# Writing the gate's x half into PSUM on ScalarE, with another order of steps and another tail

## The chip, the cores and the metric

The kernel runs on one core of a Trainium2 chip. The metric is the device time of one execution in microseconds; smaller is better. Engines are named as in the profile: PE is TensorE's matmul, PEld its weight load, DVE is VectorE, ACT is ScalarE, POOL is GpSimd, SP is SyncE, which issues all transfers here.

## What is computed

A batch of 8 sequences of 100 rows attends over 722 context rows, a gate mixes the result into x, and an RMS norm closes. All is float32.

```python
memory_proj = jnp.einsum('bme,de->bmd', memory, W_mem)                 # 8 x 722 x 1024
scores = jnp.einsum('bnd,bmd->bnm', hidden_states, memory_proj) / jnp.sqrt(jnp.float32(D))
attn = jax.nn.softmax(scores, axis=-1)
memory_context = jnp.einsum('bnm,bmd->bnd', attn, memory_proj)         # 8 x 100 x 1024
gate_input = jnp.concatenate([hidden_states, memory_context], axis=-1)
gate = jax.nn.sigmoid(jnp.einsum('bnf,df->bnd', gate_input, W_gate) + b_gate)
fused = hidden_states + gate * memory_context
return _rmsnorm(fused, norm_w)
```

## The kernel before

Features lie on partitions (8 tiles of 128), the 800 rows (8 x 100) on columns. Every float32 product is made as three matmuls of rounded operands: high by high, high by low, low by high (`three`, L287). ScalarE makes each high part, VectorE the low part.

The program has four parts. First q is made from x (L310). Then `step` (L365) runs once per batch: scores, softmax, the transposed probabilities, the context product, and between them, to fill PE's waits, the x half of the gate for feature tile b (`gate_x`, L355), which is saved to `acc[:, b, :]` (`save_gate`, L603 on ScalarE, L794 on VectorE). Then `mc_block` (L431) makes the memory context mc. Last comes the gate phase, which the change is about.

**The gate phase** goes through a written list `STEPS` (L30), (feature tile t, first column, last column): first (0, 0, 512) and (0, 512, 800), then tiles 1 to 7 of columns 0 to 512, then tiles 1 to 7 of columns 512 to 800. There are 16, numbered 0 to 15; `LAST` is 15, and `END0` is 8, the last with 512 columns. I call steps 9 to 15 the late ones. In each:

- PE (`gate_mc`, L455) makes the mc half with 24 matmuls into PSUM bank 4 or 5 in turn.
- VectorE (`gate_sum`, L866) adds the x half from `acc` and writes `gate`; ScalarE (`sigmoid`, L679) applies the sigmoid in place; VectorE multiplies by mc (`gate_times`, L872) and adds x (`fuse`, L878), which writes `acc`.
- ScalarE (`finish`, L694) squares the result and multiplies it by the norm's weight (`weigh`); VectorE (`sum_squares`, L859) adds the squares up.
- PE's step n waits for `gate_summed` of step n-2, since it uses that bank again (L460).

Step 15 is an exception. Its x half was never saved: the last batch's `gate_x` left columns 512 to 800 in PSUM bank 7 (`GLB`, `keep=True`), and PE adds to it there.

The weights of tile t+2 are split into high and low parts at step t (`SPLIT_AT`, `split_gate_w`). For the first 512 columns the norm's factor is spread over the partitions by two small PE jobs inside steps 10 and 11 (`mean_first`, `inverse`), and VectorE applies it in `output` (L890), two tiles in each of steps 11 to 14. The output of the late columns is turned on PE in three chunks of 96 rows (`turn`, L490; 8 transposes each), since they leave the chip as rows. Then follow their means (L512, L513), the root on POOL (L954), the scaling into rows on ScalarE and VectorE (L719, L938) and three transfers (L280).

Of the kernel before, what the change touches and what calls it, by code (L numbers as in the profile page):

```python
# [5 lines left out]
B, N, D = 8, 100, 1024  # L6
# [15 lines left out]


# [6 lines left out]
STEPS = [(0, 0, FIRST), (0, FIRST, R)] + [(t, 0, FIRST) for t in range(1, KD)] \  # L30
# [9 lines left out]
def build(nc, xT, ctxT, ctxN, w_mem, w_gate_x, w_mem_t, w_gate_mc, b_gate, norm_w, outT, out_rows):  # L40
# [4 lines left out]
    with top:  # L45
# [73 lines left out]
        G2B, RIB, GLB = 4, 3, 7  # L119
# [4 lines left out]
        def gate_bank(n):  # L124
            r0, r1 = STEPS[n][1:]
            return bank(G2B + n % 2, r1 - r0) if n < LAST else bank(GLB, r1 - r0, P, r0 - FIRST)
# [43 lines left out]
        gate_summed = sem("gate_summed")  # L170
# [115 lines left out]
        def _(pe):  # L286
# [68 lines left out]
            def gate_x(slot, k0, k1, keep):  # L355
                for k in range(k0, k1):
                    if keep:
                        outs = [bank(GXB, FIRST), bank(GLB, R - FIRST)]
                        stream = [(act_hi[:, k, r0:r1], act_lo[:, k, r0:r1]) for r0, r1 in ((0, FIRST), (FIRST, R))]
                    else:  # L360
                        outs, stream = [bank(GXB, H), bank(GXB + 1, H)], halves(act_hi, act_lo, k)
                    last = three(outs, w_tile(slot, k), stream, k == 0, k == KD - 1)
                return last

            def step(b, slot, cuts, keep=False):  # L365


                def fill(i):
                    if cuts[i] < cuts[i + 1]:
                        last = gate_x(slot, cuts[i], cuts[i + 1], keep)  # L370
                        if cuts[i + 1] == KD:
                            last.then_inc(w_used, 1)
# [75 lines left out]
            pe.wait_ge(gx_saved, 2 * B - 1)  # L448
# [6 lines left out]
            def gate_mc(n, after=None, work=None):  # L455

                t, r0, r1 = STEPS[n]
                pe.wait_ge(w_lo_done, J_G2 + 1 + t)
                if 2 <= n < LAST:
                    pe.wait_ge(gate_summed, n - 1)  # L460
                for k in range(KD):
                    if n == 0:
                        pe.wait_ge(mc_lo_done, k + 1)
                    done = three([gate_bank(n)], w_tile(W_HOME[t], k), [(act_hi[:, k, r0:r1], act_lo[:, k, r0:r1])],
                                 k == 0 and n < LAST, k == KD - 1, onto=n == LAST)
                    if k == after:
                        work()
                done.then_inc(gate_made, 1)
# [21 lines left out]
            def turn(i, t0, t1):  # L490

                at = FIRST + i * CHUNK
                for t in range(t0, t1):
                    done = nc.tensor.transpose(bank(2 * i + t // 4, P, CHUNK, t % 4 * P), acc[:, t, at:at + CHUNK],
                                               ident[:, :])
                return done
# [9 lines left out]
            pe.wait_ge(out_done, KD)  # L506
            turn(1, 0, KD - 1)
            turn(2, 0, KD - 1)
# [8 lines left out]
            for i in range(ROWS2):  # L517
                turn(i, KD - 1, KD).then_inc(turned, 1)
# [3 lines left out]
        def _(act):  # L522
# [84 lines left out]
            def step(b, slot, more):  # L607
# [25 lines left out]
                if not more:  # L633
                    act.wait_ge(w_used, J_GX + 1 + b)
                    nc.scalar.activation(acc[:, b, 0:FIRST], bank(GXB, FIRST), ACT.Copy).then_inc(gx_saved, 1)
# [25 lines left out]
            def split_gate_w(t):  # L661
# [4 lines left out]
                else:  # L666
                    free = (gate_made, 2)
# [11 lines left out]
            def sigmoid(n):  # L679
                t, r0, r1 = STEPS[n]  # L680
                part = gate[:, n % 2, 0:r1 - r0]
                if n < LAST:
                    act.wait_ge(gate_summed, n + 1)
                else:
                    act.wait_ge(gate_made, n + 1)
                nc.scalar.activation(part, part if n < LAST else gate_bank(n), ACT.Sigmoid,  # L686
                                     bias=bias_t[:, t:t + 1]).then_inc(gate_done, 1)

# [14 lines left out]

            for n in range(LAST + 1):
                if n in SPLIT_AT:
                    split_gate_w(SPLIT_AT[n])
                if n == END0 + 1 or n == LAST:
                    finish(n - 1)
                    sigmoid(n)
                else:  # L710
                    sigmoid(n)
                    if n > 0:
                        finish(n - 1)
            act.wait_ge(late_squared, 1)
            weigh(LAST)
            for i in range(ROWS2):
                act.wait_ge(late_rooted, 1)
                act.wait_ge(turned, i + 1)
                nc.scalar.activation(row_out[:, i * D:i * D + BANK], bank(2 * i, BANK, CHUNK), ACT.Copy,  # L719
# [4 lines left out]
        def _(dve):  # L724
# [74 lines left out]
            def step(b, slot, more):  # L799
# [18 lines left out]
                if more:  # L818
# [3 lines left out]
                      q_hi[:, :, bass.ds(b * N, N)]).then_inc(at_lo_done, 1)  # L822
                if more:
# [81 lines left out]
            gate_sum(END0 + 1)  # L905
# [5 lines left out]
            gate_sum(END0 + 2)  # L911
            sum_squares(END0 + 1)
            gate_times(END0 + 2)
            fuse(END0 + 2)
# [20 lines left out]
            for i in range(ROWS2):  # L935
                dve.wait_ge(late_rooted, 1)
                dve.wait_ge(turned, i + 1)
                nc.vector.tensor_scalar(row_out[:, i * D + BANK:(i + 1) * D], bank(2 * i + 1, BANK, CHUNK),  # L938
# [47 lines left out]
```

## Time and profile before

| | before |
|---|---|
| median of 3 runs | 306.95 us (306.56 to 307.0) |
| profiled execution | 307.06 us |
| its span | 305.3 us |
| around the span | 1.76 us |
| PE busy | 293.8 us, 96% |
| DVE busy | 171.4 us, 56% |
| ACT busy | 150.9 us, 49% |
| DMA share of the 16 engines, queue 1 | 44.1% |

The span is what the trace shows from the first to the last instruction. PE is busy from 4 us to 289 us with no gap that counts, so the remaining idle time lies at the two ends. A row of the timeline gives start, length (from first start to last end for several instructions), engine, line and operation, then in brackets how long the engine was idle before it and who ended that.

### The profile page before, as it was taken

What the parts mean: (1) busy time and instruction counts of PE and PEld (TensorE: products, weight loads), DVE (VectorE), ACT (ScalarE), POOL (GpSimd) and SP (SyncE); (2) the same over time, 40 slices, a digit from 0 to 9 for tenths busy, and PEclk for the clock granted to TensorE, in tenths of its full rate; (3) what the DMA queues carried; (4) which work ended last, traced back from release to release, by engine and by line L of the source; (5) the groups of instructions that cost most, each with busy time, mean ns of one, the idle gap of its engine ahead of it and who ended that gap; (6) DMA issues with size and microseconds to landing.
All of it is one profiled execution on the core that took longest, in us unless ns stands there. A gap on an engine that the chain in (4) does not pass through costs nothing.

```text
span 305.3 us, 4189 instructions
## 1 busy us (share of the span) xinstructions
PE 293.8 (96%) x1647; PEld 272.4 (89%) x1647; DVE 171.4 (56%) x248; ACT 150.9 (49%) x217; POOL 2.6 (1%) x8
## 2 busy tenths in 40 slices
PE   8999999999999999999999999999999999999970
PEld 7999999898989989898998889999888888899860
DVE  2758555566675656668565514433474673466752
ACT  5638337473654837365483515554554452435322
POOL 0000000000000000000000000000000000010000
PEclk9999999999999999999999999999999999999976
DMA  6996382625828295482824102292143200001325
GB/s 211 402 402 217 128 316 77 202 104 157 292 84 275 109 266 190 153 292 77 280 110 163 49 19 71 92 409 76 61 144 133 70 0 1 2 0 46 138 93 155
DMA packets 18352, 46.31 MB, mean 152 GB/s; under 512 B 1520, under 2 KB 2288, under 8 KB 18336
## 3 DMA queue, kind: packets, MB, share of 16 engines
q1 hardware_dynamic: 18336, 46.09, 44.1%
q8 instruction: 11, 0.18, 0.2%
q14 instruction: 5, 0.04, 0.0%
HBM read 42.80 MB, written 3.28 MB: 151 GB/s over the span
## 4 chain that ended last, share of the span: by engine, by line
PE 86%; issue 8%; DVE 2%; ACT 1%; DMA 1%; DVEq 0%; POOL 0%; POOLq 0%
PE ps L292 61%; PE ps L408 11%; PE ps L384 10%; PE ps L398 1%; PE ps L415 1%; DMA acc<-xT 1%; PE ps L317 0%; DVE square_sum L864 0%; ACT gate L686 0%; DVEq L45 0%; DVE gate L869 0%; DVE acc L881 0%; POOL rms L952 0%; PE ps L320 0%; POOLq L45 0%
## 5 line engine op out<-in xcount | busy, mean ns | idle before, releaser
L292 PE MATMUL ps<-act_hi,w_hi 128*128 128x400 f32 (+2 forms) x268 | 79.4, 347 | 0.0
L292 PE MATMUL ps<-act_hi,w_lo 128*128 128x400 f32 (+2 forms) x268 | 78.7, 344 | 0.0
L292 PE MATMUL ps<-act_lo,w_hi 128*128 128x400 f32 (+2 forms) x268 | 78.7, 344 | 0.0
L292 PEld LDWEIGHTS ps<-act_hi,w_hi 128*128 128x128 f32 x268 | 49.0, 188 | 3.2 <-DVE act_lo L726 0.2
L292 PEld LDWEIGHTS ps<-act_lo,w_hi 128*128 128x128 f32 x268 | 49.4, 188 | 2.2
L292 PEld LDWEIGHTS ps<-act_hi,w_lo 128*128 128x128 f32 x268 | 49.4, 188 | 2.1
L726 DVE TENSOR_TENSOR w_lo<-w_stage,w_hi 128x1024 fp32r<-128x1024 f32 (+2 forms) x23 | 26.0, 1131 | 22.8 <-ACT w_hi L530 21.5
L726 DVE TENSOR_TENSOR cn_lo<-cn_stage,cn_hi 128x1536 fp32r<-128x1536 f32 (+2 forms) x24 | 28.6, 1217 | 5.3 <-ACT cn_hi L549 5.2
L686 ACT ACTIVATE gate<-gate,bias_t 128x512 f32<-128x512 f32 (+1 forms) x15 | 9.6, 637 | 38.4 <-DVE gate L869 38.4
L726 DVE TENSOR_TENSOR ct_lo<-ct_stage,ct_hi 128x1444 fp32r<-128x1444 f32 x16 | 25.8, 1653 | 0.5 <-ACT ct_hi L541 0.5
L530 ACT ACTIVATE w_hi<-w_stage 128x1024 fp32r<-128x1024 f32 x20 | 21.0, 1054 | 8.2 <-PE ps L292 6.2
L625 ACT ACTIVATE pc<-ps,row_inv 100x512 f32<-100x512 f32 x8 | 5.5, 689 | 33.9 <-PE ps L408 33.9
L541 ACT ACTIVATE ct_hi<-ct_stage 128x1444 fp32r<-128x1444 f32 x16 | 21.7, 1408 | 0.0
L384 PE MATMUL ps<-ct_hi,qb_hi 128*100 128x362 f32 x64 | 21.4, 334 | 0.0
L384 PE MATMUL ps<-ct_lo,qb_hi 128*100 128x362 f32 x64 | 21.0, 328 | 0.0
L384 PE MATMUL ps<-ct_hi,qb_lo 128*100 128x362 f32 x64 | 21.0, 328 | 0.0
L609 ACT ACTIVATE probs<-ps,neg_top 100x722 f32<-100x722 f32 x8 | 6.9, 866 | 27.2 <-DVE neg_top L804 27.2
L726 DVE TENSOR_TENSOR act_lo<-mc,act_hi 128x800 fp32r<-128x800 f32 x8 | 8.0, 994 | 20.4 <-ACT mc L658 20.4
L408 PE MATMUL ps<-cn_hi,pt_hi 128*100 128x512 f32 (+1 forms) x48 | 18.9, 394 | 0.0
L408 PE MATMUL ps<-cn_hi,pt_lo 128*100 128x512 f32 (+1 forms) x48 | 18.9, 394 | 0.0
L408 PE MATMUL ps<-cn_lo,pt_hi 128*100 128x512 f32 (+1 forms) x48 | 18.9, 393 | 0.0
L869 DVE TENSOR_TENSOR gate<-ps,acc 128x512 f32<-128x512 f32 (+1 forms) x15 | 8.7, 580 | 17.1 <-PE ps L292 17.1
(99 smaller groups left out, 449.0 us busy)
## 6 DMA issues: line engine op xcount, KB each, us to landing
ct_stage<-ctxT SPq DMA_DIRECT2D x16, 722.0 KB, 9.4
cn_stage<-ctxN SPq DMA_DIRECT2D x8, 768.0 KB, 5.5
cn_stage<-ctxN SPq DMA_DIRECT2D x8, 512.0 KB
w_stage<-w_gate_x SPq DMA_DIRECT2D x8, 512.0 KB, 8.0
w_stage<-w_gate_mc SPq DMA_DIRECT2D x8, 512.0 KB, 3.5
x_again<-xT SPq DMA_DIRECT2D x1, 3200.0 KB, 11.7
acc<-xT SPq DMA_DIRECT2D x6, 400.0 KB, 7.1
w_stage<-w_mem_t SPq DMA_DIRECT2D x4, 512.0 KB, 5.5
```

The lines of the kernel that those rows point to most:

```text
L292: done = nc.tensor.matmul(o, wgt, stream[h][part], start=first and wgt is wh and part == 0, stop=last and wgt is wl, skip_group_check=onto)
L384: done = nc.tensor.matmul(bank(h, MH + 1, N), lhs[:, k, :], rhs[:, k, at:at + MH + 1], start=k == 0 and part == 0, stop=k == KC - 1 and pa ...
L398: done = nc.tensor.transpose(o, probs[:, t * P:t * P + rows], ident[0:N, 0:N])
L408: done = nc.tensor.matmul(bank(PCB, C, N), lhs[0:rows, t, :], rhs[0:rows, t, :], start=t == 0 and part == 0, stop=t == MT and part == 2)
L415: done = nc.tensor.transpose(bank(PTB5, N, P, c * N), pc[:, c * P:(c + 1) * P], ident[0:N, 0:N])
L530: nc.scalar.activation(w_hi[home][:, :], w_stage[:, slot, :], ACT.Copy).then_inc(w_hi_done, 1)
L541: nc.scalar.activation(ct_hi[:, 2 * s:2 * s + 2, :], ct_stage[:, 2 * s:2 * s + 2, :], ACT.Copy).then_inc(ct_hi_done, 1)
L609: nc.scalar.activation(probs[:, :].rearrange("p (h m) -> p h m", h=2), scores, ACT.Exp, bias=neg_top[:, :], scale=float(D) ** -0.5, accum_ ...
L625: nc.scalar.activation(pc[:, :], bank(PCB, C, N), ACT.Copy, scale=row_inv[:, :]).then_inc(pc_scaled, 1)
L686: nc.scalar.activation(part, part if n < LAST else gate_bank(n), ACT.Sigmoid, bias=bias_t[:, t:t + 1]).then_inc(gate_done, 1)
L726: return nc.vector.tensor_tensor(out, whole, hi.bitcast(F32), ALU.subtract)
L869: nc.vector.tensor_tensor(gate[:, n % 2, 0:r1 - r0], gate_bank(n), acc[:, t, r0:r1], ALU.add).then_inc(gate_summed, 1)
```

## The change

1. **The seed.** For steps 2 to 15, ScalarE copies the x half `acc[:, t, r0:r1]` into the PSUM bank (`seed`), and PE's 24 matmuls add to it (the first has `start=False`). VectorE's `gate_sum` stays for steps 0 and 1 only. The sigmoid of steps 2 to 15 reads PSUM and writes `gate`; it waits for `gate_made` and for `fused` of two steps before. PE's step n waits for `seeded` of its bank. `seed(n+2)` stands on ScalarE behind `sigmoid(n)`.
2. **Step order.** (1, 0, 512) comes second and (0, 512, 800) third, so both banks are written over their full 512 columns by a matmul group that starts fresh, before the first seed.
3. **The last batch.** `gate_x` is the same for all batches, bank 7 is no longer kept, tile 7 is saved by both engines, and PE's loop covers batches 2 to 7 in three turns, where it covered 2 to 5 in two, with 6 and 7 written out.
4. **VectorE's order.** `fuse(n)` comes before `sum_squares(n-1)`.
5. **The tail.** Chunk 1 is turned into banks 2 and 7 and chunk 2 into banks 4 and 3 (`TURN`). Only chunk 2 waits for `out_done`. All 8 transposes of chunk 2 stand behind the means.

```diff
-STEPS = [(0, 0, FIRST), (0, FIRST, R)] + [(t, 0, FIRST) for t in range(1, KD)] \
+STEPS = [(0, 0, FIRST), (1, 0, FIRST), (0, FIRST, R)] + [(t, 0, FIRST) for t in range(2, KD)] \
     + [(t, FIRST, R) for t in range(1, KD)]
...
+TURN = ((0, 1), (2, 7), (4, 3))
...
-            with pe.Fori(1, B // 2 - 1) as i:
+            with pe.Fori(1, B // 2) as i:
                 step(2 * i, 0, CUTS)
                 step(2 * i + 1, 1, CUTS)
-            step(B - 2, 0, CUTS)
-            step(B - 1, 1, CUTS, keep=True)
...
-            pe.wait_ge(gx_saved, 2 * B - 1)
+            pe.wait_ge(gx_saved, 2 * B)
...
-                if 2 <= n < LAST:
-                    pe.wait_ge(gate_summed, n - 1)
+                if n >= 2:
+                    pe.wait_ge(seeded, n - 1)
...
-                                 k == 0 and n < LAST, k == KD - 1, onto=n == LAST)
+                                 k == 0 and n < 2, k == KD - 1, onto=n >= 2)
...
             pe.wait_ge(weighted, LAST)
             turn(0, 0, KD - 1)
-            pe.wait_ge(out_done, KD)
             turn(1, 0, KD - 1)
-            turn(2, 0, KD - 1)
             pe.wait_ge(summed, LAST)
             pe.wait_ge(late_squared, 1)
...
             pe.wait_ge(weighted, LAST + 1)
-            for i in range(ROWS2):
-                turn(i, KD - 1, KD).then_inc(turned, 1)
+            turn(0, KD - 1, KD).then_inc(turned, 1)
+            turn(1, KD - 1, KD).then_inc(turned, 1)
+            pe.wait_ge(out_done, KD)
+            turn(2, 0, KD).then_inc(turned, 1)
...
-                if n < LAST:
+                if n < 2:
                     act.wait_ge(gate_summed, n + 1)
                 else:
+                    act.wait_ge(fused, n - 1)
                     act.wait_ge(gate_made, n + 1)
...
+            def seed(n):
+                t, r0, r1 = STEPS[n]
+                act.wait_ge(gate_done, n - 1)
+                nc.scalar.activation(gate_bank(n), acc[:, t, r0:r1], ACT.Copy).then_inc(seeded, 1)
...
             for n in range(END0 + 1):
-                gate_sum(n)
+                if n < 2:
+                    gate_sum(n)
                 if n in SPLIT_AT:
                     split_gate_w(SPLIT_AT[n])
                 gate_times(n)
+                fuse(n)
                 if n > 0:
                     sum_squares(n - 1)
-                fuse(n)
...
-            for n in range(END0 + 3, LAST):
-                gate_sum(n)
-                sum_squares(n - 1)
+            for n in range(END0 + 2, LAST):
                 gate_times(n)
                 fuse(n)
+                sum_squares(n - 1)
```

VectorE's row of instructions from step 13 to step 14, before (the line is that of its kernel, then output and inputs, shape and waits; `acc<-acc,ps` is `output`):

```order
L869 TENSOR_TENSOR gate<-ps,acc 128x288 [waits gate_made]
L864 TENSOR_TENSOR square_sum<-square_sum,square 128x288 [waits summed,squared]
L876 TENSOR_TENSOR gate<-gate,mc 128x288 [waits gate_done]
L881 TENSOR_TENSOR acc<-gate,x_again 128x288 [waits gated]
L893 TENSOR_TENSOR acc<-acc,ps 128x512 x2
L869 TENSOR_TENSOR gate<-ps,acc 128x288 [waits gate_made]
```

And the same steps on VectorE now:

```order
L881 TENSOR_TENSOR gate<-gate,mc 128x288 [waits gate_done]
L886 TENSOR_TENSOR acc<-gate,x_again 128x288 [waits gated]
L869 TENSOR_TENSOR square_sum<-square_sum,square 128x288 [waits summed,squared]
L898 TENSOR_TENSOR acc<-acc,ps 128x512 x2
L881 TENSOR_TENSOR gate<-gate,mc 128x288 [waits gate_done]
```

The sum over PSUM is gone, and the sum of squares now stands between `fuse` and the two outputs.

ScalarE's row from step 13 to step 15 now (`ps<-acc` is the last seed, that of step 15; before, L689's row was not there and each sigmoid read `gate` and waited for `gate_summed`):

```order
L683 ACTIVATE gate<-ps,bias_t 128x288 [waits gate_made,fused]
L689 ACTIVATE ps<-acc 128x288 [waits gate_done]
L702 ACTIVATE square<-acc 128x288 [waits summed,fused]
L693 ACTIVATE acc<-acc,norm_t 128x288 [waits squared]
L683 ACTIVATE gate<-ps,bias_t 128x288 [waits gate_made,fused]
L702 ACTIVATE square<-acc 128x288 [waits summed,fused]
L693 ACTIVATE acc<-acc,norm_t 128x288 [waits squared]
L702 ACTIVATE square<-acc 128x288 [waits summed,fused]
L693 ACTIVATE acc<-acc,norm_t 128x288 [waits squared]
L683 ACTIVATE gate<-ps,bias_t 128x288 [waits gate_made,fused]
```

One copy per step is added there, and it stands ahead of the squares of the step before.

PE's tail before (`ps<-ident,acc` are the transposes, `ps<-mean_w,...` the means):

```order
L494 MATMUL ps<-ident,acc 96x128 [waits weighted]
L494 MATMUL ps<-ident,acc 96x128 x6
L494 MATMUL ps<-ident,acc 96x128 [waits out_done]
L494 MATMUL ps<-ident,acc 96x128 x13
L512 MATMUL ps<-mean_w,square_sum 96x1 [waits late_squared,summed]
```

And now, from the same point:

```order
L490 MATMUL ps<-ident,acc 96x128 [waits weighted]
L490 MATMUL ps<-ident,acc 96x128 x13
L506 MATMUL ps<-mean_w,square_sum 96x1 [waits late_squared,summed]
```

Fourteen transposes stand ahead of the means instead of 21, and the wait for the outputs is gone from there.

## Rows read from the trace of the kernel before

**Rows 1.** The page: busy time, share, instructions; PE's granted clock in 40 slices.

```profile
PE 293.8 (96%) x1647; PEld 272.4 (89%) x1647; DVE 171.4 (56%) x248; ACT 150.9 (49%) x217; POOL 2.6 (1%) x8
PEclk9999999999999999999999999999999999999976
```

**Rows 2.** Timeline of PE, end of the gate phase: steps 14 and 15, first transposes.

```profile
286.09 0.30 PE L292 MATMUL ps<-act_hi,w_hi 128*128 128x288 f32 x1
...
289.16 0.29 PE L292 MATMUL ps<-act_hi,w_lo 128*128 128x288 f32 x1
291.97 1.30 PE L494 MATMUL ps<-ident,acc 128*96 128x128 f32 x8 [2.52 <-ACT acc L691]
```

**Rows 3.** Timeline of DVE, step 13 up to the sum of step 14.

```profile
284.35 0.45 DVE L869 TENSOR_TENSOR gate<-ps,acc 128x288 f32<-128x288 f32 x1
285.74 0.46 DVE L864 TENSOR_TENSOR square_sum<-square_sum,square 128x288 f32<-128x288 f32 x1 [0.94 <-ACT square L700]
286.11 0.45 DVE L876 TENSOR_TENSOR gate<-gate,mc 128x288 f32<-128x288 f32 x1
286.60 0.46 DVE L881 TENSOR_TENSOR acc<-gate,x_again 128x288 f32<-128x288 f32 x1
286.97 1.28 DVE L893 TENSOR_TENSOR acc<-acc,ps 128x512 f32<-128x512 f32 x2
288.17 0.45 DVE L869 TENSOR_TENSOR gate<-ps,acc 128x288 f32<-128x288 f32 x1
```

**Rows 4.** Timeline of ACT, late steps: a sigmoid with its square, then step 15's.

```profile
284.83 0.54 ACT L686 ACTIVATE gate<-gate,bias_t 128x288 f32<-128x288 f32 x1 [2.38 <-DVE gate L869]
285.28 0.43 ACT L700 ACTIVATE square<-acc 128x288 f32<-128x288 f32 x1
...
291.82 0.48 ACT L686 ACTIVATE gate<-ps,bias_t 128x288 f32<-128x288 f32 x1
```

**Rows 5.** Timeline of the tail: DVE's last products, PE's means, the root's result used.

```profile
293.33 0.46 DVE L932 TENSOR_TENSOR square<-acc 128x288 f32<-128x288 f32 x1
...
295.83 0.37 PE L512 MATMUL ps<-mean_w,square_sum 128*96 128x1 f32 x2
...
296.75 0.31 PE L513 MATMUL ps<-mean_w,square 128*96 128x1 f32 x2
...
297.10 0.16 DVE L934 TENSOR_SCALAR rms_late<-ps 96x3 f32<-96x3 f32 x1 [3.31 <-PE ps L513]
...
298.22 2.06 DVE L938 TENSOR_SCALAR x_again<-ps,rms_late 96x512 f32<-96x512 f32 x3 [0.97 <-POOL rms_late L954]
```

**Rows 6.** Windows: us, busy time of PE, PEld, DVE, ACT, POOL, granted clock, DMA share, GB/s.

```profile
291.90:292.90 1.00, 0.93 (x8) 0.93 (x9) 0.96 (x4) 0.41 (x2) 0.00 (x0) 0.89 0.00 0
292.90:293.40 0.50, 0.50 (x4) 0.48 (x3) 0.47 (x2) 0.00 (x0) 0.00 (x0) 0.50 0.86 336
...
295.80:296.40 0.60, 0.60 (x8) 0.60 (x7) 0.00 (x0) 0.00 (x0) 0.00 (x0) 0.75 0.00 0
```

**Rows 7.** Line 494: duration ns min/median/max; then two stretches of PE's timeline.

```profile
L494 PE MATMUL ps<-ident,acc x24: 272/421/421, 292.0 to 297.2; 128*96 128x128 f32 x24
...
293.06 1.06 PE L494 MATMUL ps<-ident,acc 128*96 128x128 f32 x4
...
296.93 0.51 PE L494 MATMUL ps<-ident,acc 128*96 128x128 f32 x3
```

**Rows 8.** The chain in order of time: start, us, what; the scores of batches 3 and 4.

```profile
93.52 3.97 PE ps L384 x24
...
111.27 4.14 PE ps L384 x24
```

**Rows 9.** Timeline, start of the gate phase: tile 1's low part, PE's step 1, step 0's sigmoid.

```profile
219.89 1.23 DVE L726 TENSOR_TENSOR w_lo<-w_stage,w_hi 128x1024 fp32r<-128x1024 f32 x1
222.76 0.29 PE L292 MATMUL ps<-act_hi,w_hi 128*128 128x288 f32 x1
...
223.79 0.72 ACT L686 ACTIVATE gate<-gate,bias_t 128x512 f32<-128x512 f32 x1 [2.99 <-DVE gate L869]
```

More of the change, by code:

```diff
@@ L118, in build @@
         GXB, PTB, PTB5, PCB = 2, 4, 5, 6
-        G2B, RIB, GLB = 4, 3, 7
+        G2B, RIB = 4, 3
         def late_mean(i, n=1):
@@ L169, in build @@
         mc_saved = sem("mc_saved")
-        gate_summed = sem("gate_summed")
+        gate_summed, seeded = sem("gate_summed"), sem("seeded")
         gate_done = sem("gate_done")
@@ L353, in _, with gate_x, step @@
                     done.then_inc(w_used, 1)
-            def gate_x(slot, k0, k1, keep):
+            def gate_x(slot, k0, k1):
                 for k in range(k0, k1):
[L357 to L362, printed above, removed]
+                    last = three([bank(GXB, H), bank(GXB + 1, H)], w_tile(slot, k),
+                                 halves(act_hi, act_lo, k), k == 0, k == KD - 1)
                 return last
-            def step(b, slot, cuts, keep=False):
+            def step(b, slot, cuts):
                 def fill(i):
                     if cuts[i] < cuts[i + 1]:
-                        last = gate_x(slot, cuts[i], cuts[i + 1], keep)
+                        last = gate_x(slot, cuts[i], cuts[i + 1])
                         if cuts[i + 1] == KD:
@@ L493, in turn @@
                 for t in range(t0, t1):
-                    done = nc.tensor.transpose(bank(2 * i + t // 4, P, CHUNK, t % 4 * P), acc[:, t, at:at + CHUNK],
+                    done = nc.tensor.transpose(bank(TURN[i][t // 4], P, CHUNK, t % 4 * P), acc[:, t, at:at + CHUNK],
                                                ident[:, :])
@@ L634, in step @@
                     act.wait_ge(w_used, J_GX + 1 + b)
-                    nc.scalar.activation(acc[:, b, 0:FIRST], bank(GXB, FIRST), ACT.Copy).then_inc(gx_saved, 1)
+                    save_gate(b)
                 if more:
@@ L666, in split_gate_w @@
                 else:
-                    free = (gate_made, 2)
+                    free = (gate_made, 3)
                 split_w(J_G2 + t, t % 2, free, W_HOME[t])
@@ L681, in sigmoid @@
                 part = gate[:, n % 2, 0:r1 - r0]
-                if n < LAST:
+                if n < 2:
                     act.wait_ge(gate_summed, n + 1)
                 else:
+                    act.wait_ge(fused, n - 1)
                     act.wait_ge(gate_made, n + 1)
-                nc.scalar.activation(part, part if n < LAST else gate_bank(n), ACT.Sigmoid,
+                nc.scalar.activation(part, part if n < 2 else gate_bank(n), ACT.Sigmoid,
                                      bias=bias_t[:, t:t + 1]).then_inc(gate_done, 1)
+            def seed(n):
+                t, r0, r1 = STEPS[n]
+                act.wait_ge(gate_done, n - 1)
+                nc.scalar.activation(gate_bank(n), acc[:, t, r0:r1], ACT.Copy).then_inc(seeded, 1)
             def weigh(n):
@@ L702, in finish @@
                 weigh(n)
+            act.wait_ge(gx_saved, 2 * B)
             for n in range(LAST + 1):
@@ L708, in _ @@
                     finish(n - 1)
[L709 to L713, printed above, removed]
+                sigmoid(n)
+                if n + 2 <= LAST:
+                    seed(n + 2)
+                if n > 0 and n not in (END0 + 1, LAST):
+                    finish(n - 1)
             act.wait_ge(late_squared, 1)
@@ L822, in step @@
                       q_hi[:, :, bass.ds(b * N, N)]).then_inc(at_lo_done, 1)
+                if not more:
+                    save_gate(b)
                 if more:
```

11 lines of the change are left out of this document (3 added, 8 removed).

## The prediction

> **What bounds the kernel now.** I read the page first. PE is busy for 96% of the span, and its granted clock is at 90% or more in 38 of 40 slices [rows 1]. So up to the end of the gate phase only PE's own work counts, and nothing that is taken from VectorE there is worth anything directly. The last two slices, where the clock falls, are the place to look at.
>
> The timeline of PE shows it [rows 2]. Step 15's last matmul starts at 289.16 and ends at 289.45. The next instruction of PE, the first transpose, starts at 291.97, and ScalarE's weighing of step 14 (`weighted`) released it. PE had been idle for 2.5 us. So ScalarE and VectorE are late there, not PE.
>
> Why they are late is seen in one late step on VectorE [rows 3]. From the sum at 284.35 to the next sum at 288.17 it takes 3.82 us. PE takes 289.16 - 286.09 = 3.07 us for 23 starts, so 3.20 us for a step of 24 [rows 2]. VectorE therefore falls back by 0.62 us per step once it also makes two outputs per step, and at step 14 it is 1.9 us late: PE was done at about 286.25, the sum started at 288.17. VectorE isn't full, though. It waits for 0.94 us in the step. In-order work makes the loop: sum (VectorE), sigmoid, square (ScalarE), and only then the sum of squares, at which the product and the outputs queue.
>
> From there the tail is a chain [rows 5]: step 15's sigmoid at 291.82 [rows 4], square on VectorE from 293.33 to 293.79, means on PE from 295.83, `rms_late` at 297.10, the root, the rows from 298.22, the last transfers. The means start 2.04 us after their input is there, since 21 transposes that began late stand ahead of them.
>
> **Part by part.**
>
> *VectorE per late step.* The sum and the loop through ScalarE go. What is left, as distances of starts [rows 3]: product to `fuse` 0.49, `fuse` 0.37, sum of squares 0.37, two outputs 1.20. That is 2.43 us, below PE's 3.20 us. VectorE now starts each step when the sigmoid is done and waits for PE again. Its order matters once: the sum of squares needs ScalarE's square, which now stands behind a seed. Measured from the sigmoid's start, the square is done after 0.45 (sigmoid to square, [rows 4]) + 0.45 for the seed + 0.43 = 1.33 us; VectorE asks for it after 0.57 + 0.49 + 0.37 = 1.43 us. No wait.
>
> *The seed.* The trace has no ScalarE write from SBUF to PSUM. The nearest rows of 288 columns take 0.43 to 0.54 us [rows 4], and one of 512 columns takes 0.72 us [rows 9]. I take 0.45 as the distance of starts in a late step (the square's, which also has no bias); bounds are 0.4 and 0.6. Its cover: in a late step the sigmoid starts just after PE's end, and the seed must be done one PE step later: 3.20 - 0.05 - 0.45 = 2.70 us for something of 0.45. The tightest place is step 1: A step of 512 columns takes 3.20 x 512 / 288 = 5.7 us by the late step's time, so PE would end it at 222.76 + 5.7 = 228.5; then VectorE's sum (0.69) and the sigmoid (0.72) come first, so the seed of step 3 runs from 229.9 to 230.6. Step 3 starts after the 3.2 us of step 2, at 231.7. It is hidden with 1 us to spare. ScalarE's added work, 14 seeds, costs nothing.
>
> *Step order.* Tile 1's weights are now needed at 222.76 and not 3.2 us later. Their low part is done at 219.89 + 1.23 = 221.12 [rows 9], 1.6 us early. VectorE's sum of step 1 moves back to 228.5, and the split of tile 3 (1.23 us) is queued behind it; it ends by 230.5, and step 4 wants it after one more step of 512 columns, at 237.4. The load of tile 5 waits for that split and so starts near 230.5; step 6 wants it two steps on, at 248.8. Both are hidden.
>
> *Last batch.* Both ways of cutting the 800 columns keep the same sum of columns, so PE gains nothing. VectorE's added save of 400 columns stands where it waits for ScalarE's split anyway. The loop costs something: the scores of batch 4, the first after a jump back, take 4.14 us against 3.97 for batch 3 [rows 8]. The third turn adds one such jump: +0.17 us.
>
> *Tail, first term.* In step 14 PE ends at 286.25, so the product starts at about 286.86, and VectorE is through with the last two outputs 2.43 us later, at 289.3, and with the sum of squares at 289.66. Step 15's sigmoid is no longer held by ScalarE's finish of step 14, which is over by 288.8 (`fuse` ends at 286.86 + 0.49 + 0.46 = 287.8, square 0.43, weighing about 0.54). It starts with PE's end, at 289.49, and not at 291.82 [rows 4]: -2.33 us. Its product can start at 290.0, 0.35 us after VectorE is free. From sigmoid to the end of the square it is 293.79 - 291.82 = 1.97 us as before, so the square is ready at 291.46.
>
> *Tail, second term.* The transposes need step 14 weighed, which is true at 288.8. They start at 289.4 with no gap. At the full clock three of them take 0.51 us with 0.272 for one, so they are 0.12 us apart [rows 7]; 14 need 1.7 us and end by 291.2, before the square. The means start at about 291.6, 0.15 us after the square, where it was 2.04 us: -1.9 us.
>
> *Tail, third term.* The six means took 296.75 + 0.31 - 295.83 = 1.23 us with their first part at the half clock [rows 5, 6]. At the full clock I expect 1.15: -0.1 us. The rest (root, three rows on two engines, transfers) is as before. The 10 transposes behind the means need 10 x 0.12 = 1.2 us, so the last rows' input is there by 294.1; it is wanted after the root (298.22 - 297.10 = 1.12) and two of three rows (2.06 x 2/3 = 1.4), near 295.3 [rows 5]. Hidden by about 1 us.
>
> *Sum.* 305.3 - 2.33 - 1.9 - 0.1 + 0.17 = 301.15 us of span. With 1.76 us around it that is 302.9, and the profiled execution was 0.1 above the median: **302.8 us**.
>
> **Rivals.**
>
> *The clock falls in the tail.* Before, the granted clock was at its half level (1.2 GHz) in the window 292.9 to 293.4, after PE had stood still for 2.5 us, and it was rising again in the window 295.8 to 296.4, when PE had done nothing but transposes since [rows 6]. In the new tail PE stands still for only about 0.4 us, ahead of the means, so I expect the full level throughout. If it fell at the first transpose, they would be (1.06 - 0.421) / 3 = 0.213 us apart [rows 7], 14 would take 3.0 us and end at 292.5, 0.9 us after 291.6, and the six means would cost some 0.3 us more: 304.0 us. The Trainium skill ("TensorE: Matmul & The Clock Gate", Part 4: PE-mode transpose) says that the full clock doesn't engage for transposes, since they don't count as busy in the same way. By that rule this is the case that comes; the row in which the clock rises during transposes speaks against it.
>
> *VectorE stays late.* If the seed pushed the square back so far that VectorE's step still took 3.8 us, only the transposes would move ahead. That spares 1.9 us and no more, and gives 305.1 us. It needs a seed that is longer by 1.3 us or more; every ScalarE row of this width speaks against it.
>
> *Slower: PE waits for seeds.* PE has never had to wait in the gate phase, and now each step from 2 on hangs on one instruction of an in-order engine. The place is the late steps, six of them with a seed (10 to 15), where the cover is 2.7 us. The gain above is 4.1 us, so it turns to a loss when each seed comes more than 0.7 us too late, that is takes over 3.4 us, say because ScalarE's writes to PSUM are held while PE writes to it. At 3.6 us it would be 6 x 0.9 = 5.4 us, thus 302.8 + 5.4 = 308.2 us. The longest ScalarE row of that width is 0.54 us.
>
> *The last rows' transposes bind.* They stand behind the means now. They have about 1 us of cover, and even at the half clock they take 2.1 us and come about when they are wanted: 302.8 to 303.0 us, inside the forecast.
>
> **How the numbers follow.** The forecast has 0.82. The clock case has 0.07, VectorE late 0.04, the slower case 0.03, and 0.04 are for what I have not seen. The range goes down to 302.2: the transfers at the end, read from one execution, and the seeds' lower bound allow some 0.6 us. Upward it takes in the clock case, 304.0, with 0.2 us for the run's own spread: 302.2 to 304.2. A difference within 0.2% is about what a measurement of this kernel cannot tell from none; that is 0.6 us. Faster by more than that: 0.95; within: 0.02; slower: 0.03.
>
> **What would show it.** In the timeline of the changed kernel PE should go from step 15's last matmul to the first transpose with no idle time, and the wait on ScalarE's weighing should be gone. The two outputs of step 14 should end before step 15's sigmoid. Product to product on VectorE should be 3.2 us in late steps, set by PE. Before the means there should be a short wait (about 0.4 us) for VectorE's square, and the granted clock should stay full until the means are done. The seeds should take 0.4 to 0.6 us with no wait of PE on ScalarE's new line. I am wrong if PE waits for `seeded`, if the clock falls during the transposes, or if step 15's sigmoid still starts more than 0.2 us after PE's end.

## The result and the profile after

The changed kernel takes 303.06 us, the median of four executions (302.82 to 303.27). The kernel before takes 306.75 us in the same comparison (305.69 to 307.0); its executions fall into two groups, which e11 below explains. The ratio is 0.9886, with a 95% interval of 0.9859 to 0.9913. The prediction was 302.8 us, range 302.2 to 304.2.

The profiled execution took 303.27 us with a span of 301.5 us, so 1.77 us lie around the span (before: 1.76). The page of the changed kernel answers [rows 1]:

```profile
PE 292.5 (97%) x1647; PEld 272.2 (90%) x1647; DVE 166.5 (55%) x236; ACT 157.4 (52%) x231; POOL 2.6 (1%) x8
PEclk9999999999999999999999999999999999999996
```

VectorE has 12 instructions less and ScalarE 14 more. One slice at the lower clock is left, where there were two, and PE's last instruction ends at 294.43 us, near the start of that slice.

PE's waits in the changed kernel (who waited for whom, total us, times, longest us):

```profile
PE ps L308 <- DVE idle_work L754: 1.0, 1, 1.0
PE ps L506 <- DVE square L932: 0.7, 1, 0.7
PE ps L319 <- ACT w_hi L557: 0.2, 1, 0.2
```

The 2.5 us for ScalarE's weighing is gone, and there is no wait for a seed. The wait of 1.0 us is at the start of the kernel and was there before. PE's timeline at the end of step 15 answers [rows 2]:

```profile
289.63 0.29 PE L294 MATMUL ps<-act_hi,w_lo 128*128 128x288 f32 x1
289.77 1.69 PE L490 MATMUL ps<-ident,acc 128*96 128x128 f32 x14
292.15 0.30 PE L506 MATMUL ps<-mean_w,square_sum 128*96 128x1 f32 x2 [0.69 <-DVE square L932]
...
293.16 1.27 PE L490 MATMUL ps<-ident,acc 128*96 128x128 f32 x10
```

The transposes follow the last matmul with no gap, and 14 of them take 1.69 us. VectorE's late step answers [rows 3], here step 13 and the product of step 14:

```profile
284.16 0.46 DVE L881 TENSOR_TENSOR gate<-gate,mc 128x288 f32<-128x288 f32 x1 [0.68 <-ACT gate L683]
284.65 0.46 DVE L886 TENSOR_TENSOR acc<-gate,x_again 128x288 f32<-128x288 f32 x1
285.03 0.45 DVE L869 TENSOR_TENSOR square_sum<-square_sum,square 128x288 f32<-128x288 f32 x1
285.40 1.28 DVE L898 TENSOR_TENSOR acc<-acc,ps 128x512 f32<-128x512 f32 x2
287.36 0.46 DVE L881 TENSOR_TENSOR gate<-gate,mc 128x288 f32<-128x288 f32 x1 [0.68 <-ACT gate L683]
```

From product to product it is 3.20 us (284.16 to 287.36), as long as a step of PE, and VectorE waits 0.68 us in it for the sigmoid. The lag no longer adds up. ScalarE's timeline answers [rows 4]:

```profile
283.63 0.50 ACT L683 ACTIVATE gate<-ps,bias_t 128x288 f32<-128x288 f32 x1 [1.31 <-PE ps L294]
284.16 0.42 ACT L689 ACTIVATE ps<-acc 128x288 f32<-128x288 f32 x1
284.51 0.43 ACT L702 ACTIVATE square<-acc 128x288 f32<-128x288 f32 x1
...
290.03 0.50 ACT L683 ACTIVATE gate<-ps,bias_t 128x288 f32<-128x288 f32 x1 [0.66 <-PE ps L294]
```

The sigmoid of step 15 starts 0.11 us after PE's end of that step (289.63 + 0.29 = 289.92). Before, it started 2.37 us after PE's end (291.82 - 289.45). VectorE's tail answers [rows 5]:

```profile
289.79 0.45 DVE L869 TENSOR_TENSOR square_sum<-square_sum,square 128x288 f32<-128x288 f32 x1
290.56 0.46 DVE L881 TENSOR_TENSOR gate<-gate,mc 128x288 f32<-128x288 f32 x1 [0.31 <-ACT gate L683]
...
291.55 0.46 DVE L932 TENSOR_TENSOR square<-acc 128x288 f32<-128x288 f32 x1
293.34 0.16 DVE L934 TENSOR_SCALAR rms_late<-ps 96x3 f32<-96x3 f32 x1 [1.33 <-PE ps L507]
294.46 2.06 DVE L938 TENSOR_SCALAR x_again<-ps,rms_late 96x512 f32<-96x512 f32 x3 [0.96 <-PE ps L490]
```

The window that answers [rows 6] (us, busy PE, PEld, DVE, ACT, POOL, granted clock, DMA share, GB/s) is at the full level (2.4 GHz) throughout:

```profile
289.80:293.10 3.30, 2.61 (x27) 2.38 (x26) 1.82 (x5) 1.04 (x2) 0.00 (x0) 1.00 0.41 159
```

**Where the time went.** I compare the two spans by stages. From the end of step 15's matmuls to `rms_late` it was 297.10 - 289.45 = 7.65 us and is 293.34 - 289.92 = 3.42 us: -4.23 us. From there to the end nothing changed (8.2 us in both). Up to the end of step 15 the new profile is 0.47 us later. Of that, 0.17 us is the loop on PE, and the rest is there before any changed line runs. The chain shows both. Each row gives start, length and what ran: PE's stretch of q, then the scores of batch 6, first before, then after.

```profile
7.43 35.00 PE ps L292 x192
...
146.95 3.99 PE ps L384 x24
```

```profile
7.80 34.94 PE ps L294 x192
...
147.29 4.16 PE ps L382 x24
```

PE's stretch of q begins at 7.80 us and not at 7.43. That start differs between executions without any changed line ahead of it: it lies between 6.89 us (e3) and 7.80 us in the profiles of all runs. The scores of batch 6 now take 4.16 us, where they took 3.99 us, as the prediction said for one more jump back.

### The profile page after: what moved, and what is told of

The parts are those of the page before. It is cut to its first block, busy times and chain, and to the rows that moved or that the text cites. A ratio compares the mean times of both kernels' runs of the same rounds, so it can differ in the third digit from the quotient of the medians.

```text
span 301.5 us, 4214 instructions
## 1 busy us (share of the span) xinstructions
PE 292.5 (97%) x1647; PEld 272.2 (90%) x1647; DVE 166.5 (55%) x236; ACT 157.4 (52%) x231; POOL 2.6 (1%) x8
## 4 chain that ended last, share of the span: by engine, by line
PE 96%; DMA 1%; DVE 1%; ACT 0%; DVEq 0%; issue 0%; ACTq 0%
PE ps L294 69%; PE ps L406 11%; PE ps L382 11%; PE ps L396 1%; PE ps L413 1%; DMA acc<-xT 1%; PE ps L319 0%; DVEq L47 0%; PE ps L490 0%; PE ps L322 0%; PE ps L325 0%; PE ps L478 0%; PE ps L470 0%; DVE x_again L938 0%; PE ps L506 0%
## 5 line engine op out<-in xcount | busy, mean ns | idle before, releaser
L683 ACT ACTIVATE gate<-ps,bias_t 128x288 f32<-128x288 f32 (+1 forms) x14 | 8.1, 579 | 24.2 <-PE ps L294 24.2
L881 DVE TENSOR_TENSOR gate<-gate,mc 128x512 f32<-128x512 f32 (+1 forms) x16 | 9.2, 573 | 20.0 <-ACT gate L683 20.0
```

Source lines behind the costliest of these rows:

```text
L683: nc.scalar.activation(part, part if n < 2 else gate_bank(n), ACT.Sigmoid, bias=bias_t[:, t:t + 1]).then_inc(gate_done, 1)
L881: nc.vector.tensor_tensor(part, part, mc[:, t, r0:r1], ALU.mult).then_inc(gated, 1)
```

## The experiments

The questions were: how much came from the seeds, from VectorE's order, from the tail and from the clock; and how large the cover of a seed is. "Before" in each comparison is the kernel before, on the same chip. There are three comparisons, each on a chip of its own: e1, e2, e3 and e8 (before: 306.71 us); e4, e6, e10 and e11 (306.81 us); e5, e7 and e9 (306.51 us). e7, e9 and e10 are one execution each.

**e1: the changed kernel with the old tail.**

```diff
             turn(0, 0, KD - 1)
+            pe.wait_ge(out_done, KD)
             turn(1, 0, KD - 1)
+            turn(2, 0, KD - 1)
...
-            turn(0, KD - 1, KD).then_inc(turned, 1)
-            turn(1, KD - 1, KD).then_inc(turned, 1)
-            pe.wait_ge(out_done, KD)
-            turn(2, 0, KD).then_inc(turned, 1)
+            for i in range(ROWS2):
+                turn(i, KD - 1, KD).then_inc(turned, 1)
```

> The changed kernel with the old order of transposes: chunk 0, the wait for the outputs, chunks 1 and 2 (21 transposes) ahead of the means, the last feature tile of all three behind. Theory A (the gain came from VectorE no longer being late, so that step 15's sigmoid starts with PE's end and the transposes run early and at the full clock): the transposes start at about 289.8, 21 x 0.12 = 2.5 us, the means start at 292.3 to 292.5 instead of 292.15, time 303.2 to 303.5. Theory B (the new order of the tail carries the second half of the gain, 1.9 us): 304.5 to 305.

Measured: 303.07 us, ratio 0.9884 (0.9860 to 0.9909), the same as the changed kernel. PE's timeline:

```profile
289.22 2.46 PE L490 MATMUL ps<-ident,acc 128*96 128x128 f32 x21
291.60 0.30 PE L508 MATMUL ps<-mean_w,square_sum 128*96 128x1 f32 x2
```

PE ends step 15 at 289.38 here, the square ends at 291.46, and 21 transposes at full clock end just in time: the means start 0.14 us after the square. So taking seven transposes out of the way brings nothing once they start in time. Theory B falls.

**e2: the kernel before with the new tail alone** (`TURN = ((0, 1), (2, 4), (5, 3))`, and the lines of e1 the other way round).

> The kernel before with the new order of the tail alone (chunk 1 into banks 2 and 4, chunk 2 into banks 5 and 3, all of chunk 2 behind the means). Theory A: PE still stands idle for 2.5 us until 291.97, the clock falls in the transposes as before, 7 at 0.12 and 7 at 0.213 us end by 294.4; the means start there instead of 295.83: -1.4 us, 305.3. Theory B: the means start right behind the square at 293.9, -1.9 us or more, 304.8.

Measured: 305.92 us (304.68 to 306.37), ratio 0.9977 (0.9957 to 0.9998). The profiled execution took 304.95 us:

```profile
291.86 1.73 PE L495 MATMUL ps<-ident,acc 128*96 128x128 f32 x14 [2.52 <-ACT acc L692]
293.82 0.30 PE L511 MATMUL ps<-mean_w,square_sum 128*96 128x1 f32 x2 [0.23 <-DVE square L933]
```

PE's 2.52 us of idle time is unchanged. In this execution the clock stayed full, and 14 transposes took 1.73 us, where theory A expected 2.4. The median misses both theories (305.3 and 304.8). The ten executions are of two kinds: three with a mean granted clock of 0.990 or 0.991 took 304.68 to 304.97 us, seven with 0.981 to 0.986 took 305.50 to 306.37 us. That led to e11: the clock seems to fall behind that wait in some executions and not in others. The new tail is worth 0.7 us where it falls (median 306.03 against 306.76 us of before) and 0.25 us where it does not (304.95 against 305.20).

**e11: the kernel before with PE kept busy through the wait.** Nothing reads what the added matmuls write.

```diff
+            for _ in range(40):
+                nc.tensor.matmul(bank(2, P), idle_work[:, :], idle_work[:, :], start=True, stop=True)
             pe.wait_ge(weighted, LAST)
```

> The kernel before, with 40 small matmuls on PE between step 15 and the wait for ScalarE's weighing, where it stood idle for 2.5 us; nothing reads them. Theory G (part of what the change gained is the clock: in the profile of before it fell to the half level behind that idle time and the transposes ran at 0.213 instead of 0.12 us): the clock stays full, 21 transposes take 2.5 us from 291.97, the means start at 294.5 instead of 295.8, and every run is near 305.3. If the clock didn't matter: 306.7 as before.

Measured: 305.23 us, ratio 0.9959 (0.9937 to 0.9981). The timeline of this kernel, then the transposes of the kernel before:

```profile
289.14 2.41 PE L505 MATMUL ps<-idle_work 128*128 128x128 bf16 x40
291.82 2.50 PE L494 MATMUL ps<-ident,acc 128*96 128x128 f32 x21 [0.28 <-ACT acc L693]
```

```profile
291.97 4.07 PE L494 MATMUL ps<-ident,acc 128*96 128x128 f32 x21 [2.52 <-ACT acc L691]
```

Theory G holds. The transposes are released as late as before, 2.53 us after PE's end of step 15, but 21 of them take 2.50 us, where they took 4.07 us; the granted clock is 1.00 in the whole tail up to the last transpose. The means start 0.51 us after the square, where it was 2.04 us.

The kernel before has executions of two kinds. In the three comparisons, 13 with a mean granted clock of 0.990 or 0.991 took 304.98 to 305.65 us (median 305.28), and 26 with 0.980 to 0.986 took 306.43 to 307.73 us (median 306.88). In e11 all ten have 0.991 or more and take 304.90 to 306.06 us. So the fallen clock costs 1.6 us, and filling the idle time prevents it. The changed kernel has 0.69 us of idle time in place of 2.52, and its four executions have 0.990 or more.

**e3: the kernel before with VectorE's new order alone.** No seed, old tail. The order is changed in the late steps: in step 10, which stands ahead of this loop, and in the loop of steps 11 to 14.

```diff
                 gate_sum(n)
-                sum_squares(n - 1)
                 gate_times(n)
                 fuse(n)
+                sum_squares(n - 1)
```

> The kernel before, with VectorE's sum over PSUM kept and no seed, but in the late steps the sum of squares behind the product and fuse (and behind the old tail). Theory A (what made VectorE late was mostly its order: it waited 0.94 us for the square ahead of the product): a late step takes 0.48 + 0.56 + 0.49 + 0.37 + 0.37 + 1.20 = 3.47 us instead of 3.82, the lag at the end is about 0.8 us instead of 1.9, the product of step 15 starts near 290.9 instead of 292.35, the means near 292.8 instead of 295.83, time 303.7. Rival C (only taking the sum off VectorE brings the step below PE's 3.20 us, and with any lag the tail stays as it was): 305.5 or more.

Measured: 303.66 us, ratio 0.9904 (0.9879 to 0.9930). VectorE's step 14, its product of step 15, and PE's transposes:

```profile
286.95 0.45 DVE L869 TENSOR_TENSOR gate<-ps,acc 128x288 f32<-128x288 f32 x1
288.00 0.46 DVE L876 TENSOR_TENSOR gate<-gate,mc 128x288 f32<-128x288 f32 x1 [0.60 <-ACT gate L686]
...
290.80 0.45 DVE L876 TENSOR_TENSOR gate<-gate,mc 128x288 f32<-128x288 f32 x1
```

```profile
290.05 2.50 PE L494 MATMUL ps<-ident,acc 128*96 128x128 f32 x21 [0.81 <-ACT acc L691]
```

From the sum at 286.95 to 290.44, where VectorE is through with the two outputs of step 14, it is 3.49 us (expected 3.47). That is still more than PE's 3.20 us, so the lag is smaller and not gone: step 15's sigmoid starts 0.67 us after PE's end. PE's idle time shrinks from 2.5 to 0.8 us, and the clock stays full, so these 3.05 us hold the 1.6 us of the clock too. Moving one instruction, with no seed, gives 3.05 of the 3.7 us. Rival C falls.

**e8: the kernel before with the new order and the new tail**, e3 and e2 together.

> The kernel before, no seed, with VectorE's new order in the late steps and the new order of the tail. Theory A: the product of step 15 near 290.9, the means right behind the square, near 292.5: 303.4 to 303.6, so the seeds themselves are worth about 0.5 us of the change. Rival C: the seeds carry the gain, 305 or more.

Measured: 303.73 us, ratio 0.9906 (0.9880 to 0.9932), 0.1 to 0.3 us above what was expected and no better than e3. The tail brings nothing here either. What is left for the seeds is 0.6 us, and it has to carry the loop's 0.17 us too. e1 and e3, on one chip and both with the old tail, give it as 303.66 - 303.07 us; no execution of the one (302.86 to 303.12) reaches those of the other (303.40 to 303.89). The traces agree roughly: from PE's end of step 15 to `rms_late` it is 293.58 - 289.23 = 4.35 us in e3 and 292.79 - 289.38 = 3.41 us in e1, 0.94 us less, and the loop takes back 0.17 us.

**e4: the changed kernel with the old order on VectorE in steps 10 to 14**, seeds kept.

```diff
+                sum_squares(n - 1)
                 gate_times(n)
                 fuse(n)
-                sum_squares(n - 1)
```

> The changed kernel, with the sum of squares ahead of the product in the late steps, as before the change. Theory D (the seed frees ScalarE from VectorE: sigmoid n starts with PE's end of step n whatever VectorE is at, so VectorE's wait for the square no longer repeats a lag): VectorE starts its 2.43 us of work 1.4 us after PE's end, is through 3.85 us after it, which is before it can start the next (3.2 + 1.4), and step 15's product comes less than 0.1 us later: 303.1. Theory E (the order decides, with or without the seed, and a step costs 3.8 us again): step 15's product 1.5 us late, 304.6.

Measured: 302.93 us, ratio 0.9898 (0.9857 to 0.9939). VectorE's timeline, steps 13 and 14, then ScalarE's sigmoids of steps 14 and 15:

```profile
285.17 0.46 DVE L869 TENSOR_TENSOR square_sum<-square_sum,square 128x288 f32<-128x288 f32 x1 [0.69 <-ACT square L702]
...
287.89 0.46 DVE L869 TENSOR_TENSOR square_sum<-square_sum,square 128x288 f32<-128x288 f32 x1 [0.20 <-ACT square L702]
```

```profile
287.02 0.50 ACT L683 ACTIVATE gate<-ps,bias_t 128x288 f32<-128x288 f32 x1 [1.32 <-PE ps L294]
...
290.22 0.50 ACT L683 ACTIVATE gate<-ps,bias_t 128x288 f32<-128x288 f32 x1
```

Theory D holds. With the seeds the order doesn't matter for the time. VectorE again waits for the square ahead of its product, but the sigmoid of step 14 waits for PE and not for VectorE, so a lag of VectorE isn't handed on to the next step. Ahead of step 15's sigmoid ScalarE does wait 0.82 us for VectorE's `fuse` of step 14, and the sigmoid still starts 0.10 us after PE's end (290.12). Order and seed are two cures of one illness, a loop through both engines, and either one is enough for most of the gain. The seed does two things at once: it frees the sigmoid from VectorE, and it takes the sum (0.48 us per step) off VectorE. No run separates the two.

**e6 and e10: longer seeds.** The six late seeds are written four times (e6) or eight times (e10), each write behind the last. The edit is that of e6; in e10 both 3s are 7s.

```diff
+                for i in range(3 if n > END0 + 1 else 0):
+                    nc.scalar.activation(gate_bank(n), acc[:, t, r0:r1], ACT.Copy).then_inc(padded, 1)
+                    act.wait_ge(padded, (n - END0 - 2) * 3 + i + 1)
```

> Each of the six late seeds is written four times, one after the other, about 1.7 us in all. The prediction's rival (VectorE late, from a seed of 1.3 us on, the lag adding up over the steps, 305.1 us). Theory D: the lag is a constant 0.6 us, since ScalarE no longer waits for VectorE's sum, and step 14 has no seed; step 15's product is 0.2 us late, PE never waits: 303.3.

Measured: 303.47 us (303.16 to 303.90), ratio 0.9913 (0.9881 to 0.9945). VectorE's timeline: the product of step 13, its wait for the square in that step, and the products of steps 14 and 15.

```profile
284.91 0.45 DVE L884 TENSOR_TENSOR gate<-gate,mc 128x288 f32<-128x288 f32 x1
...
286.53 0.46 DVE L872 TENSOR_TENSOR square_sum<-square_sum,square 128x288 f32<-128x288 f32 x1 [0.68 <-ACT square L705]
...
288.10 0.45 DVE L884 TENSOR_TENSOR gate<-gate,mc 128x288 f32<-128x288 f32 x1
...
290.90 0.45 DVE L884 TENSOR_TENSOR gate<-gate,mc 128x288 f32<-128x288 f32 x1
```

From product to product it is 3.19 us, and in steps 13 and 14 alike the product starts 0.55 us after the sigmoid's end: a lag that does not add up. In step 15 it is 0.15 us (290.25 + 0.50 to 290.90), where the changed kernel has 0.03 us. So seeds that are 1.3 us longer (1.76 us from 284.38 to 286.14) cost 0.1 us in the tail of the profile and 0.4 us in the medians, which come from different comparisons.

> Each of the six late seeds is written eight times, about 3.5 us in all. PE must wait for seeds now. By the prediction's reckoning (cover of 2.7 us, the excess of each seed counts) 6 x 0.8 = 5 us: 308. Theory F (ScalarE's whole queue bounds it: sigmoid 0.5, seeds 3.5, square and weighing 0.9, so 4.9 us per late step instead of 3.2, and both finishes of steps 7 and 8 between the first two seeds): PE waits five times by 1 to 2.6 us, 9 us in sum: 312.

Measured: 313.62 us. PE's waits, then ScalarE's timeline of step 13:

```profile
PE ps L294 <- ACT ps L692: 7.1, 5, 1.7
```

```profile
292.10 0.48 ACT L683 ACTIVATE gate<-ps,bias_t 128x288 f32<-128x288 f32 x1
292.62 3.10 ACT L690 ACTIVATE ps<-acc 128x288 f32<-128x288 f32 x7
295.75 0.41 ACT L692 ACTIVATE ps<-acc 128x288 f32<-128x288 f32 x1
296.10 0.43 ACT L705 ACTIVATE square<-acc 128x288 f32<-128x288 f32 x1
```

From sigmoid to sigmoid (287.21, 292.10, 297.00) it is 4.9 us, as theory F has it. PE ends step 15 at 299.74, 9.8 us later than the changed kernel, though it began step 9 0.2 us earlier. F had put down 9 us of waits, and the waits for seeds are 7.1 us. F left the rest out. In step 11, behind the longest wait (1.72 us), the granted clock is at its half level (window, then busy PE, PEld, DVE, ACT, POOL, granted clock, DMA share, GB/s):

```profile
277.00:279.00 2.00, 2.00 (x10) 2.00 (x10) 0.76 (x2) 1.87 (x5) 0.00 (x0) 0.50 0.03 8
```

There PE's matmuls start 0.24 us apart and not 0.133, which costs 1.3 us over 12 of them. The waits of 1.28 us ahead of step 10 and of 1.12, 1.47 and 1.47 us ahead of steps 13 to 15 left the clock at 1.00. The remaining 1.6 us are a short wait for VectorE in step 10 and PE's slower restart behind each wait. In the tail, step 15's product waits behind VectorE for 0.4 us. F's time was 1.6 us too low. The prediction's reckoning by the seed alone, 308 us, was too low by more than 5 us.

**e7: 56 more transposes ahead of the means**, nothing else on PE.

```diff
             turn(1, 0, KD - 1)
+            for _ in range(8):
+                turn(1, 0, KD - 1)
```

> The changed kernel with chunk 1 transposed eight times more ahead of the means, 56 transposes that change nothing. If transposes keep the clock up as the trace of before suggests (it rose while PE did nothing else): full clock throughout, 56 x 0.12 = 6.7 us less the idle 0.7 us, 309. If transposes don't count as busy: the granted clock falls to half among them, most of them take 0.213 us, and the time is 313 or more.

Measured: 308.43 us. PE's transposes (duration ns min/median/max) and three windows, columns as in e10:

```profile
L490 PE MATMUL ps<-ident,acc x80: 272/273/292, 289.7 to 299.3; 128*96 128x128 f32 x80
```

```profile
291.00:293.00 2.00, 2.00 (x21) 2.00 (x20) 0.91 (x2) 0.54 (x1) 0.00 (x0) 1.00 0.54 206
...
295.00:297.00 2.00, 2.00 (x20) 2.00 (x19) 0.00 (x0) 0.00 (x0) 0.00 (x0) 1.00 0.00 0
297.00:299.00 2.00, 2.00 (x24) 2.00 (x23) 0.16 (x1) 0.00 (x0) 0.28 (x1) 1.00 0.00 0
```

Seventy transposes in a row, 7.8 us with nothing else on PE, leave the granted clock at 1.00. They are 0.11 us apart, a little less than the 0.12 that I had expected, so the time is 0.6 us below the expectation.

**e9: the changed kernel with the old order of steps.**

```diff
-STEPS = [(0, 0, FIRST), (1, 0, FIRST), (0, FIRST, R)] + [(t, 0, FIRST) for t in range(2, KD)] \
+STEPS = [(0, 0, FIRST), (0, FIRST, R)] + [(t, 0, FIRST) for t in range(1, KD)] \
```

> The changed kernel with the old order of steps: (0, 512, 800) second, (1, 0, 512) third. The bank of steps 1, 3, 5 then has only columns 0 to 287 written by the group that starts fresh, so this kernel may leave out the x half of the gate in columns 288 to 511 of those steps. The time says what the order of steps costs: by the prediction nothing, 303.0; if the earlier need of tile 1's weights or the moved split of tile 3 had cost something, less.

Measured: 302.91 us, within the executions of the changed kernel (302.82 to 303.27). The order of steps costs no time that shows, as predicted. Only the time of this version is of use: as the expectation says, it may leave out part of the gate's x half.

**e5: a version beyond both.** The first halves of the means need nothing of step 15, so they can run in PE's 0.7 us of idle time. PE's loop is cut back to two turns.

```diff
-            with pe.Fori(1, B // 2) as i:
+            with pe.Fori(1, B // 2 - 1) as i:
                 step(2 * i, 0, CUTS)
                 step(2 * i + 1, 1, CUTS)
+            step(B - 2, 0, CUTS)
+            step(B - 1, 1, CUTS)
...
             pe.wait_ge(summed, LAST)
-            pe.wait_ge(late_squared, 1)
             for i in range(ROWS2):
-                nc.tensor.matmul(late_mean(i), late_sums(i), mean_w[:, :], start=True, stop=False)
+                nc.tensor.matmul(late_mean(i), late_sums(i), mean_w[:, :], start=i == 0, stop=False,
+                                 skip_group_check=True)
+            pe.wait_ge(late_squared, 1)
+            for i in range(ROWS2):
                 done = nc.tensor.matmul(late_mean(i), square[:, LAST % 2, i * CHUNK:(i + 1) * CHUNK], mean_w[:, :],
-                                        start=False, stop=True)
+                                        start=False, stop=True, skip_group_check=True)
```

> The changed kernel, with the three means' first halves (over the sum of squares of steps 9 to 14) ahead of PE's wait for step 15's square and only the three second halves behind it, and with PE's loop as before the change (two turns, the last two batches written out). The chain behind the square loses three of six small matmuls, 3 x 0.17 = 0.5 us, since PE is idle for 0.7 us there; the loop gives back 0.17 us: 302.4. If the wait only moves (PE was idle because it had to be), 302.9 to 303.1.

Measured: 302.04 us (301.74 to 302.38), ratio 0.9864 (0.9834 to 0.9894). The timeline:

```profile
290.43 0.59 PE L507 MATMUL ps<-mean_w,square_sum 128*96 128x1 f32 x6
291.19 0.67 PE L511 MATMUL ps<-mean_w,square 128*96 128x1 f32 x6 [0.17 <-DVE square L936]
```

From the end of the square to `rms_late` it is 291.90 - 291.14 = 0.76 us, where the changed kernel has 293.34 - 292.01 = 1.33 us: 0.57 us less. The scores of batch 6 take 3.99 us again, so with the loop's 0.17 us that is 0.7 us. The medians differ by 1.0 us; the intervals of the two ratios overlap, and they come from different comparisons. So 0.7 us is shown by the two stretches of the profile, and the other 0.3 us is not explained.

## Why the prediction was right, point by point

- **What bounds the kernel.** Right. Up to the end of step 15 only the start and the loop moved, and the gain came from behind PE's end.
- **VectorE's late step below PE's.** Right: 3.20 us from product to product. VectorE's own work in it, from the product's start to the outputs' end, is 286.68 - 284.16 = 2.52 us; I took 2.43 from the starts.
- **The cause of the lag.** I put it down to the loop of sum, sigmoid, square and sum of squares, which e3 and e4 show. But I priced the sum's removal and the order as one term. They are substitutes: order alone gives 303.66 us (e3), seeds with the old order 302.93 us (e4), both 303.06 us.
- **The seed at no cost.** Right in a late step: 0.35 us from its start to the square's (I took 0.45), 0.42 us long. With 512 columns it is 0.60 us long. The seed of step 3 ended at 230.57 + 0.60 = 231.17, and PE started step 3 at 232.11: the 1 us to spare was there.
- **Tail, first term, -2.33 us.** It was -2.26 us (sigmoid 0.11 us after PE's end, before 2.37).
- **Tail, second term, -1.9 us.** The size was right: the means start 0.14 us after the square. The reason was only half named. I wrote that 21 transposes stand ahead, begun late. e1 shows that their number is worth nothing when they start in time. With the clock kept up (e11) the means start 0.51 us after the square, so 1.53 of the 1.9 us were the fallen clock and 0.37 us the late start. I had that fall in [rows 6] and used it for the rival, but not for the term itself. The forecast of the time hardly hangs on it: from the executions of before in which the clock stays up, the same terms give 305.28 - 2.33 - 0.37 + 0.17 = 302.75 us, as an estimate. The gain does hang on it: over those executions it is 305.28 - 303.06 = 2.2 us and not 3.7. That I had profiled an execution of the more frequent kind was luck.
- **Tail, third term, -0.1 us.** Right: from first mean to `rms_late` it is 1.19 us, and was 1.27.
- **The wait ahead of the means.** I expected about 0.4 us, it was 0.69 us. It costs nothing here, since VectorE's square ends the wait; e5 puts it to use.
- **The loop, +0.17 us.** Right, to the hundredth.
- **The clock rival.** It did not come: the granted clock is 1.00 from the first transpose to the end of the means. The row that I held against it was weaker than I said. Narrower windows of the kernel before put the rise at 296.1 us, when the means had begun (295.83), though up to them PE had done nothing but transposes. e7 is the better evidence. The Trainium skill ("TensorE: Matmul & The Clock Gate", Part 4: PE-mode transpose) says that the full clock doesn't engage for transposes; e7, whose 70 float32 transposes keep 1.00, doesn't bear it out. Its rows call them MATMUL and don't show whether they run in the mode that the page means.
- **The rival of VectorE staying late from a seed of 1.3 us on.** It did not come, and its mechanism was wrong, as e6 shows: seeds of 1.76 us cost 0.4 us at most. The lag doesn't add up there, since the next sigmoid doesn't wait for VectorE's sum.
- **The slower rival.** It did not come. PE does wait when seeds are long enough, but the price was wrong (e10). I reckoned only with the seed against its cover, and left out the square and weighing behind it in the same queue, and the clock that PE's waits can cost. ScalarE's whole step must fit into PE's.
- **The rival of the last rows' transposes.** It did not come. They end at 293.16 + 1.27 = 294.43, and the rows start at 294.46, 1.12 us after `rms_late` as before.
- **The sum.** The terms add up to 301.14 us (I wrote 301.15), against 301.5 measured. Of the missing 0.35 us, 0.30 us is the start of the kernel, which no term held. The first term was 0.07 us too large.

## What to carry to other kernels

Where two in-order engines hand a tile back and forth within each step, look for what an engine waits for ahead of work that doesn't need it. Moving that one instruction behind the work gave four fifths of the gain here (e3), before any work was moved to another engine. When a tail is priced, read the granted clock in it: an idle time of PE costs its own length, and can cost half-speed work behind it as well. Look at several executions before you put a price on that. And when work is added to an engine, add up its whole step, not the cover of the new instruction alone.

## What was not expected of the hardware

- After 2.5 us of idle time PE's granted clock fell to the half level (1.2 GHz) in the profiled execution of the kernel before, and stayed at 1.00 in that of e2. By the mean clock of each execution it fell in 26 of 39 of the kernel before, whose two groups have medians 1.6 us apart. In e10 a wait of 1.72 us was followed by the half level, and waits of 1.1 to 1.5 us were not. After 0.7 us of idle time, as in the changed kernel, it stayed at 1.00.
- Float32 transposes alone kept the granted clock at 1.00 for 7.8 us (e7).
- In the changed kernel ScalarE's copy from SBUF into PSUM takes 0.42 us for 288 columns and 0.60 for 512. The sigmoid from PSUM takes 0.50 us, where the one from SBUF took 0.54 [rows 4].
